# One exponential, one clamp and one sum over 2048 columns per attention step of a gated cross-attention and expert kernel

## The chip, the cores and the metric

The kernel runs on one core of one Trainium2 chip. The metric is the device time of one execution in microseconds. The engines are named as in the profile: PE (TensorE; PEld its weight loads), DVE (VectorE), ACT (ScalarE), POOL (GpSimd), SP (SyncE, which only issues DMAs here).

## The reference

Four sequences of 512 tokens with 256 features (`x`) attend to four contexts of 1024 rows (`ctx_1024`), with 16 heads of 64; then a mixture of four experts, two for each token, follows. Cut to what matters:

```python
q = (lat @ Wq)...                       # lat: layer norm of layer norm of x
k, v = jnp.split(ctx @ Wkv, 2, axis=-1)
k = apply_rope(k, cos, sin)
attn = jnp.einsum('bhnd,bhsd->bhns', q, k) * 64 ** -0.5
attn = jnp.clip(attn, -11.0, 11.0)
attn = jax.nn.softmax(attn, axis=-1)
out = jnp.einsum('bhns,bhsd->bhnd', attn, v)
x = x + tanh(g_xattn) * (out @ Wo + bo)
x = x + tanh(g_ffn) * experts(layernorm(x))     # top 2 of 4, exact gelu
```

All tensors are float32. The kernel takes the exponential of the scores as they are, and clamps the result between exp(-11) and exp(11), which is the same as clipping the scores before it.

## The kernel before

**Tiling.** Each of the four images `b` has four units `u` of four heads. A unit has eight steps `s`. A step treats one pair of heads (`s // 4`) and two tiles of 128 context rows (`2 * (s % 4)` and the next). Its scores are two bank groups `sc[0]` and `sc[1]`, one for each row tile `i`; each holds 128 context rows by 2 heads x 512 tokens, so 1024 columns. There are 4 x 4 x 8 = 128 steps. `c = s % 4` counts the steps of a pair of heads.

**What one step does, in the order of each engine's own program** (each engine works strictly in order; semaphores join them):

- PE (`step` in the tensor block): `score` for i = 0 and i = 1 (L1800, six matmuls each); `k_turn` (L1786), which transposes the rotated keys of the previous row tile of the next unit; `kv_make` (L1745 to L1747), which projects keys and values of one more row tile for the next unit; at c = 0 `denominators` (L1824), which needs the sums of the four steps before; at some steps the output projection or the next queries; then `values` (L1814) of the step before. In about a third of the steps (those that also transpose context or query rows, L1752) `kv_make` stands ahead of `k_turn`.
- ACT: `exps` for i = 0 and 1 (L932), then `kv_evac` (L877 `k_raw`, L878 `val`), then `k_split` (L870).
- DVE: `clamp` for i = 0 and 1 (L1159), then `rot_cos` (L1147), `k_low` (L1111), then `sums` for i = 0 and 1 (L1171 at c = 1, L1174 at c = 2 and 3, none at c = 0), with small steps of other work between and behind.
- POOL: `rotate`, which is two instructions, L716 (`rot_s`, needs `k_raw`) and L720 (the sum of both halves of the rotation, needs `rot_cos` too). The next `k_turn` on PE waits for L720.

`prob` is double buffered over the steps (`s % 2`), `sc` is not: `score` of the next step waits until the exponential has read its half. The semaphores `sc_ready`, `exp_done`, `clamped` and `summed` exist once for each half. In the last unit of the last image (`is_direct`) no sums are made; PE sums the probabilities itself.

The sums that are two instructions of 1024 columns:

```python
            def sums(b, u, s, i):
                ...
                dve.wait_ge(clamped[i], step_no(b, u, s) + 1)
                if c == 1:
                    wait(dve, den_ready, q)
                    v.tensor_tensor(acc[:, i, :], prob[:, 0, i, :], prob[:, 1, i, :], ALU.add).then_inc(summed[i], 1)
```

After the attention the experts run in 19 jobs of 256 tokens; the change touches them only in two waits.

Of the kernel before, what the change touches and what calls it, by code (L numbers as in the profile page):

```python
# [32 lines left out]
def flamingo_kernel(nc, x, ctx_in, g_xattn, g_ffn, cos, sin, lat_g, lat_b, ctx_g, ctx_b, w_q, w_kv, w_o, b_o,  # L33
# [29 lines left out]
    with ExitStack() as stack:  # L63
# [134 lines left out]
        sc = [ps("sc0", 2 * N), ps("sc1", 2 * N)]  # L198
# [65 lines left out]
        sc_ready = [sem("sc_ready0"), sem("sc_ready1")]  # L264
        exp_done = [sem("exp_done0"), sem("exp_done1")]
        clamped = [sem("clamped0"), sem("clamped1")]
        summed = [sem("summed0"), sem("summed1")]
# [592 lines left out]
        def _(act):  # L860
# [123 lines left out]
            def step(b, u, s, last):  # L984
# [3 lines left out]
                exps(b, u, s, 0)  # L988
                exps(b, u, s, 1)
# [90 lines left out]
        def _(dve):  # L1080
# [75 lines left out]
            def clamp(b, u, s, i):  # L1156

                dve.wait_ge(exp_done[i], step_no(b, u, s) + 1)
                v.tensor_scalar(prob[:, s % 2, i, :], prob[:, s % 2, i, :], EXP_LOW, EXP_HIGH,  # L1159
                                ALU.max, ALU.min).then_inc(clamped[i], 1)  # L1160

            def sums(b, u, s, i):
# [78 lines left out]
            def step(b, u, s, last):  # L1241
# [28 lines left out]
                clamp(b, u, s, 0)  # L1270
# [7 lines left out]
                clamp(b, u, s, 1)  # L1278
# [461 lines left out]
        def _(pe):  # L1740
# [48 lines left out]
            def score(b, u, s, i):  # L1789
# [6 lines left out]
                wait(pe, exp_done[i], step_no(b, u, s))  # L1796
# [5 lines left out]
                last.then_inc(sc_ready[i], 1)  # L1802

            def values(b, u, s):
                c, j, p = s % CH, s // CH, u * 2 + s // CH
                if c == 0:

                    wait(pe, o_norm, pair_no(b, p))
                for i in range(2):
                    pe.wait_ge(clamped[i], step_no(b, u, s) + 1)  # L1810
                    for g in range(4):
                        half, h = g // 2, g % 2
                        at = (2 * j + h) * DH + half * 32
                        last = mm(pv[g * 32:(g + 1) * 32, :], val[:, u % 2, 2 * c + i, at:at + 32],  # L1814
                                  prob[:, s % 2, i, h * N:(h + 1) * N], start=c == 0 and i == 0, stop=c == CH - 1 and i == 1)
# [174 lines left out]
            def hidden(n):  # L1990
# [103 lines left out]
```

## Time and profile before

| | before |
|---|---|
| median of 3 runs | 1129.91 us (1127.69 to 1133.77) |
| the profiled execution | 1131.16 us |
| its span | 1129.6 us |
| PE, DVE, ACT, POOL busy | 95%, 84%, 58%, 48% of the span |
| granted TensorE clock, mean | 0.989 of full speed |
| attention steps | about 39 to 850 us of the span |

Busy is the time in which an instruction of the engine is in flight. Times in the rows are microseconds from the start of the span, unless marked ns. The span is the time from the first to the last instruction; the execution's own time is 1.6 us longer.

### The profile page before, as it was taken

The page shows a single profiled execution, that of the slowest core. Times are in us where ns is not written, and L with a number is a line of the kernel's source. Part 1 is how long each engine was busy: PE and PEld are TensorE (multiplying, and loading weights), DVE is VectorE, ACT ScalarE, POOL GpSimd, SP SyncE. Part 2 cuts the span into 40 slices and gives each one's busy share as a digit, 9 for nine tenths or more (in the row PEclk, how much of TensorE's full clock was granted, in tenths as well). Part 3 has the DMA queues.
Part 4 walks back from the last instruction along what each step waited for, and adds up shares of the span by engine and source line. Part 5 has one row for each costly group of instructions (what it writes and reads, how often), then busy time and mean ns, then how long its engine had stood idle before and what let it go on. Part 6 is the DMA issues. An engine that isn't in the chain of part 4 may idle for free.

```text
span 1129.6 us, 22455 instructions
## 1 busy us (share of the span) xinstructions
PE 1070.9 (95%) x7949; PEld 713.9 (63%) x7949; DVE 948.4 (84%) x1772; ACT 653.1 (58%) x1259; POOL 540.6 (48%) x551
## 2 busy tenths in 40 slices
PE   5899999999999999999999999999998998799994
PEld 3556555655555565656555565655447997799994
DVE  7898999898889989898998989889976657577675
ACT  5654557655555765555566655444565764567662
POOL 7433475333427633242654334318832646555661
PEclk9999999999999999999999999999999999999998
DMA  7000010000000000000010000601353334545344
GB/s 208 13 10 11 20 38 20 11 10 11 11 19 25 24 12 10 20 10 20 20 29 10 10 14 7 202 1 54 109 192 121 140 113 132 170 151 170 113 149 142
DMA packets 59188, 72.04 MB, mean 64 GB/s; under 512 B 11579, under 2 KB 52167, under 8 KB 59080
## 3 DMA queue, kind: packets, MB, share of 16 engines
q1 hardware_dynamic: 54840, 61.30, 17.5%
q0 software_dynamic: 3360, 8.53, 2.0%
q8 instruction: 66, 1.08, 0.4%
q10 hardware_dynamic: 880, 0.79, 0.2%
q14 instruction: 42, 0.34, 0.1%
HBM read 54.84 MB, written 16.54 MB: 63 GB/s over the span
## 4 chain that ended last, share of the span: by engine, by line
PE 74%; DVE 13%; issue 5%; ACT 3%; POOL 2%; DMA 1%; SPq 0%; ACTq 0%; DVEq 0%; POOLq 0%
PE pv L1814 16%; PE sc L1800 14%; PE kv L1745 5%; PE kv L1747 5%; PE kv L1746 5%; PE sc L1745 4%; PE sc L1747 4%; PE sc L1746 4%; PE tr L1786 3%; PE mi L1745 2%; DVE acc L1174 2%; PE mi L1746 2%; PE mi L1747 2%; PE mi L1824 2%; DVE prob L1159 2%
## 5 line engine op out<-in xcount | busy, mean ns | idle before, releaser
L932 ACT ACTIVATE prob<-sc 128x1024 f32<-128x1024 f32 x256 | 249.5, 1028 | 200.4 <-PE sc L1800 197.5
L716 POOL TENSOR_TENSOR rot_s<-k_raw,sinb 128x256 f32<-128x256 f32 x128 | 112.7, 880 | 381.1 <-ACT k_raw L877 380.9
L1814 PE MATMUL pv<-prob,val 128*32 128x512 f32 x2048 | 245.5, 597 | 2.3 <-DVE recip L1193 2.3
L1159 DVE TENSOR_SCALAR prob<-prob 128x1024 f32<-128x1024 f32 x256 | 181.6, 722 | 43.9 <-ACT prob L932 42.3
L1800 PE MATMUL sc<-q_hid,w2all 64*128 64x512 f32 x1536 | 213.4, 410 | 1.2 <-DVE w2all L1139 1.2
L1800 PEld LDWEIGHTS sc<-q_hid,w2all 64*128 64x128 f32 x1536 | 135.1, 185 | 101.4 <-issue 55.1
L1174 DVE TENSOR_TENSOR acc<-acc,prob 128x1024 f32<-128x1024 f32 x120 | 177.4, 1499 | 0.0
L720 POOL TENSOR_TENSOR rot_c<-rot_c,rot_s 128x256 f32<-128x256 f32 x128 | 111.6, 872 | 37.6 <-DVE rot_c L1147 23.0
L1814 PEld LDWEIGHTS pv<-prob,val 128*32 128x32 f32 x2048 | 56.5, 109 | 111.2 <-issue 90.4
L1745 PE MATMUL kv<-w2all,acts 128*128 128x512 f32 x248 | 109.8, 443 | 2.2 <-DVE acts L1105 1.3
L1745 PE MATMUL sc<-w2all,q_hid 128*128 x304 | 89.8, 295 | 18.1 <-DVE q_hid L1647 17.4
L1747 PE MATMUL kv<-w2all,acts 128*128 128x512 f32 x248 | 98.5, 397 | 0.0
L1746 PE MATMUL kv<-w2all,acts 128*128 128x512 f32 x248 | 98.0, 395 | 0.0
L1746 PE MATMUL sc<-w2all,q_hid 128*128 x304 | 86.7, 285 | 0.0
L1747 PE MATMUL sc<-w2all,q_hid 128*128 x304 | 86.6, 285 | 0.0
L1171 DVE TENSOR_TENSOR acc<-prob 128x1024 f32<-128x1024 f32 x60 | 85.4, 1461 | 0.0
L877 ACT ACTIVATE k_raw<-kv 128x256 f32<-128x256 f32 x124 | 48.7, 392 | 53.8 <-PE kv L1747 51.4
L1147 DVE TENSOR_TENSOR rot_c<-kv,cosb 128x256 f32<-128x256 f32 x124 | 52.2, 421 | 28.5 <-ACT val L878 22.9
L1745 PEld LDWEIGHTS sc<-w2all,q_hid 128*128 128x128 f32 x304 | 58.7, 193 | 21.4 <-issue 21.2
L779 POOL TENSOR_TENSOR acts<-prob,acts 128x512 fp32r<-128x512 f32 x36 | 48.3, 1343 | 42.8 <-ACT acts L955 41.1
L1030 ACT ACTIVATE sc<-sc,c_aff 128x256 f32<-128x256 f32 x78 | 34.9, 447 | 50.6 <-PE sc L1747 50.1
L1786 PE MATMUL tr<-ident,rot_c 128*128 128x128 f32 x256 | 54.5, 295 | 8.9 <-POOL rot_c L720 8.8
(315 smaller groups left out, 2377.4 us busy)
## 6 DMA issues: line engine op xcount, KB each, us to landing
prob<-in_L_ffn_w SPq DMA_DIRECT2D x17, 1024.0 KB, 5.3
slots_x<-lat_r SPq DMA_DIRECT2D x1, 5016.0 KB, 18.8
rows<-slots_x SPq DMA_DIRECT2D x19, 264.0 KB, 4.4
rows<-in_ctx SPq DMA_DIRECT2D x32, 128.0 KB, 2.2
w_raw<-in_L_xattn_Wq SPq DMA_DIRECT2D x16, 256.0 KB, 2.7
w_raw<-in_L_xattn_Wo SPq DMA_DIRECT2D x64, 64.0 KB
acc<-in_L_ffn_w SPq DMA_DIRECT2D x16, 256.0 KB, 4.0
acc<-in_L_ffn_w SPq DMA_DIRECT2D x5, 512.0 KB
```

Source lines behind the costliest of these rows:

```text
L716: g.tensor_tensor(rot_s[:].rearrange("p (h a c) -> p h a c", h=4, a=2), kh[:, :, ::-1, :], sinb[:, t].unsqueeze(1).to_broadcast([P, 4, 2, ...
L720: g.tensor_tensor(k_rot[:], rot_c[:], rot_s[:], ALU.add).then_inc(rot, 1)
L932: a.activation(prob[:, s % 2, i, :], sc[i][:], ACT.Exp, scale=DH ** -0.5).then_inc(exp_done[i], 1)
L1159: v.tensor_scalar(prob[:, s % 2, i, :], prob[:, s % 2, i, :], EXP_LOW, EXP_HIGH, ALU.max, ALU.min).then_inc(clamped[i], 1)
L1171: v.tensor_tensor(acc[:, i, :], prob[:, 0, i, :], prob[:, 1, i, :], ALU.add).then_inc(summed[i], 1)
L1174: v.tensor_tensor(acc[:, i, :], acc[:, i, :], prob[:, s % 2, i, :], ALU.add).then_inc(summed[i], 1)
L1745: mm(dst, lhs(0), rhs(0), start=start, stop=False, **kw)
L1746: mm(dst, lhs(0), rhs(1), start=False, stop=False, **kw)
L1747: return mm(dst, lhs(1), rhs(0), start=False, stop=stop, **kw)
L1786: last = nc.tensor.transpose(tr[:, j * P:(j + 1) * P], k_rot[:, j * P:(j + 1) * P], ident[:])
L1800: last = mm(sc[i][:, h * N:(h + 1) * N], kst[rows_h, u % 2, j, lk, t * P:(t + 1) * P], q_sp[rows_h, p % 2, lq, :], start=lk + lq == 0, sto ...
L1814: last = mm(pv[g * 32:(g + 1) * 32, :], val[:, u % 2, 2 * c + i, at:at + 32], prob[:, s % 2, i, h * N:(h + 1) * N], start=c == 0 and i == ...
```

## The change

The two score halves become halves of one PSUM tensor of four banks. ACT takes one exponential over 2048 columns, which waits until both halves of the scores are there. DVE clamps 2048 columns in one instruction and adds 2048 columns in one instruction. Each of the four semaphore pairs becomes one semaphore. PE waits for the whole exponential before either half of the next scores, for the whole clamp before `values`, for the whole sum before `denominators`. In the order of DVE the merged clamp stands where the second one stood (behind the small aggregates), and the merged sum where the first one stood (ahead of `residual`).

```diff
-        sc = [ps("sc0", 2 * N), ps("sc1", 2 * N)]
+        scores = ps("scores", 4 * N)
+        sc = [scores[:, 0:2 * N], scores[:, 2 * N:4 * N]]
...
-            def exps(b, u, s, i):
-                act.wait_ge(sc_ready[i], step_no(b, u, s) + 1)
+            def exps(b, u, s):
+                act.wait_ge(sc_ready, 2 * step_no(b, u, s) + 2)
...
-                a.activation(prob[:, s % 2, i, :], sc[i][:], ACT.Exp, scale=DH ** -0.5).then_inc(exp_done[i], 1)
+                a.activation(prob[:, s % 2].rearrange("p i n -> p (i n)"), scores[:], ACT.Exp,
+                             scale=DH ** -0.5).then_inc(exp_done, 1)
...
-                exps(b, u, s, 0)
-                exps(b, u, s, 1)
+                exps(b, u, s)
...
-            def clamp(b, u, s, i):
+            def clamp(b, u, s):
+                dve.wait_ge(exp_done, step_no(b, u, s) + 1)
+                both = prob[:, s % 2].rearrange("p i n -> p (i n)")
+                v.tensor_scalar(both, both, EXP_LOW, EXP_HIGH, ALU.max, ALU.min).then_inc(clamped, 1)
...
-                    v.tensor_tensor(acc[:, i, :], prob[:, 0, i, :], prob[:, 1, i, :], ALU.add).then_inc(summed[i], 1)
+                    v.tensor_tensor(acc[:], prob[:, 0], prob[:, 1], ALU.add).then_inc(summed, 1)
...
-                    v.tensor_tensor(acc[:, i, :], acc[:, i, :], prob[:, s % 2, i, :], ALU.add).then_inc(summed[i], 1)
+                    v.tensor_tensor(acc[:], acc[:], prob[:, s % 2], ALU.add).then_inc(summed, 1)
...
-                clamp(b, u, s, 0)
                 if done_rows:
...
-                clamp(b, u, s, 1)
+                clamp(b, u, s)
...
-                sums(b, u, s, 0)
+                sums(b, u, s)
                 if s in (2, 3) and not is_first(b, u):
                     residual(*((b, u - 1) if u else (b - 1, UNITS - 1)), s - 2)
-                sums(b, u, s, 1)
...
-                wait(pe, exp_done[i], step_no(b, u, s))
+                wait(pe, exp_done, step_no(b, u, s))
...
+                pe.wait_ge(clamped, step_no(b, u, s) + 1)
                 for i in range(2):
-                    pe.wait_ge(clamped[i], step_no(b, u, s) + 1)
...
+                pe.wait_ge(summed, (pair_no(b, p) + 1) * 3)
                 for i in range(2):
-                    pe.wait_ge(summed[i], (pair_no(b, p) + 1) * 3)
```

## Rows read from the trace of the kernel before

**Rows 1.** The page: busy us, share of span and instructions of each engine.

```profile
PE 1070.9 (95%) x7949; PEld 713.9 (63%) x7949; DVE 948.4 (84%) x1772; ACT 653.1 (58%) x1259; POOL 540.6 (48%) x551
```

**Rows 2.** Busy by stretch, attention: length, PE, PEld, DVE, ACT, POOL, clock, DMA, GB/s.

```profile
39.00:245.00 206.00, 204.37 (x1468) 116.48 (x1468) 185.90 (x312) 122.12 (x231) 90.05 (x98) 1.00 0.05 15
...
450.00:655.00 205.00, 203.97 (x1476) 117.33 (x1472) 187.38 (x322) 119.61 (x226) 92.24 (x98) 1.00 0.06 17
655.00:850.00 195.00, 187.46 (x1430) 106.75 (x1430) 170.46 (x300) 103.90 (x167) 93.56 (x83) 0.99 0.28 88
```

**Rows 3.** Waits, attention (39 to 853): us in total, times, longest.

```profile
PEld tr L1752 <- DVE w2all L1111: 7.2, 6, 1.4
PE tr L1786 <- POOL rot_c L720: 5.7, 9, 1.4
```

**Rows 4.** Timeline, all engines, image 2, unit 1, steps 6 and 7: start, us, engine.

```profile
534.60 1.67 PE L1800 MATMUL sc<-q_hid,w2all 64*128 64x512 f32 x12
535.62 1.94 ACT L932 ACTIVATE prob<-sc 128x1024 f32<-128x1024 f32 x2 [2.17 <-PE sc L1800]
...
537.94 0.65 DVE L1159 TENSOR_SCALAR prob<-prob 128x1024 f32<-128x1024 f32 x1
...
538.07 0.39 ACT L877 ACTIVATE k_raw<-kv 128x256 f32<-128x256 f32 x1 [0.51 <-PE kv L1747]
...
538.53 0.74 POOL L716 TENSOR_TENSOR rot_s<-k_raw,sinb 128x256 f32<-128x256 f32 x1 [4.95 <-ACT k_raw L877]
...
539.17 0.41 DVE L1111 TENSOR_TENSOR w2all<-tr,w2all 128x256 fp32r<-128x256 f32 x1
539.42 0.73 POOL L720 TENSOR_TENSOR rot_c<-rot_c,rot_s 128x256 f32<-128x256 f32 x1
539.50 2.87 DVE L1174 TENSOR_TENSOR acc<-acc,prob 128x1024 f32<-128x1024 f32 x2
539.82 1.65 PE L1800 MATMUL sc<-q_hid,w2all 64*128 64x512 f32 x12
...
541.40 0.44 PE L1786 MATMUL tr<-ident,rot_c 128*128 128x128 f32 x2
...
542.29 1.28 DVE L1159 TENSOR_SCALAR prob<-prob 128x1024 f32<-128x1024 f32 x2
```

**Rows 5.** The page's costliest groups: busy us, mean ns of one, idle before, releaser.

```profile
L932 ACT ACTIVATE prob<-sc 128x1024 f32<-128x1024 f32 x256 | 249.5, 1028 | 200.4 <-PE sc L1800 197.5
...
L1159 DVE TENSOR_SCALAR prob<-prob 128x1024 f32<-128x1024 f32 x256 | 181.6, 722 | 43.9 <-ACT prob L932 42.3
```

**Rows 6.** Timeline of POOL, image 1, unit 2, step 1.

```profile
350.34 1.19 POOL L716 TENSOR_TENSOR rot_s<-k_raw,sinb 128x256 f32<-128x256 f32 x1
351.67 1.65 POOL L720 TENSOR_TENSOR rot_c<-rot_c,rot_s 128x256 f32<-128x256 f32 x1
```

**Rows 7.** Timeline of DVE in the same step.

```profile
349.22 1.71 DVE L1159 TENSOR_SCALAR prob<-prob 128x1024 f32<-128x1024 f32 x1
...
351.52 1.21 DVE L1171 TENSOR_TENSOR acc<-prob 128x1024 f32<-128x1024 f32 x1
```

**Rows 8.** Timeline of PE, image 2, unit 0: scores of steps 3 to 6.

```profile
463.37 1.65 PE L1800 MATMUL sc<-q_hid,w2all 64*128 64x512 f32 x12
...
470.00 1.65 PE L1800 MATMUL sc<-q_hid,w2all 64*128 64x512 f32 x12
...
476.07 1.67 PE L1800 MATMUL sc<-q_hid,w2all 64*128 64x512 f32 x12
...
482.65 1.67 PE L1800 MATMUL sc<-q_hid,w2all 64*128 64x512 f32 x12
```

**Rows 9.** Timeline of POOL, image 2, unit 0, step 7: the reciprocal root of L727.

```profile
490.02 2.25 POOL L727 TENSOR_TENSOR f_stats<-f_stats,mhalf 128x4 f32<-128x4 f32 x1
```

**Rows 10.** Timeline of PE, image 1, unit 2, step 0: scores and denominators.

```profile
340.03 1.66 PE L1800 MATMUL sc<-q_hid,w2all 64*128 64x512 f32 x12
...
343.38 1.07 PE L1824 MATMUL mi<-acc,ones 128*32 128x256 f32 x16
```

More of the change, by code:

```diff
@@ L262, in flamingo_kernel @@
         q_ready = sem("q_ready")
[L264 to L267, printed above, removed]
+        sc_ready = sem("sc_ready")
+        exp_done = sem("exp_done")
+        clamped = sem("clamped")
+        summed = sem("summed")
         pv_done = sem("pv_done")
@@ L924, in q_round @@
                 a.activation(q_sp[:, p % 2, 0, :], mi[:], ACT.Copy).then_inc(q_high, 1)
-            def exps(b, u, s, i):
-                act.wait_ge(sc_ready[i], step_no(b, u, s) + 1)
+            def exps(b, u, s):
+                act.wait_ge(sc_ready, 2 * step_no(b, u, s) + 2)
                 c, q = s % CH, pair_no(b, u * 2 + s // CH)
                 if not (is_direct(b, u) and s > 1):
-                    wait(act, summed[i], q * 3 - 1 if c == 0 else q * 3 if c == 1 else q * 3 + 1)
-                a.activation(prob[:, s % 2, i, :], sc[i][:], ACT.Exp, scale=DH ** -0.5).then_inc(exp_done[i], 1)
+                    wait(act, summed, q * 3 - 1 if c == 0 else q * 3 if c == 1 else q * 3 + 1)
+                a.activation(prob[:, s % 2].rearrange("p i n -> p (i n)"), scores[:], ACT.Exp,
+                             scale=DH ** -0.5).then_inc(exp_done, 1)
             def x_out(b, hf, bank, raw):
@@ L1154, in q_low, with sums @@
                 v.tensor_tensor(q_sp[:, p % 2, 1, :], mi[:], q_sp[:, p % 2, 0, :].bitcast(F32), ALU.subtract).then_inc(q_ready, 1)
-            def clamp(b, u, s, i):
[L1158 to L1162, printed above, removed]
+            def clamp(b, u, s):
+                dve.wait_ge(exp_done, step_no(b, u, s) + 1)
+                both = prob[:, s % 2].rearrange("p i n -> p (i n)")
+                v.tensor_scalar(both, both, EXP_LOW, EXP_HIGH, ALU.max, ALU.min).then_inc(clamped, 1)
+            def sums(b, u, s):
                 c, q = s % CH, pair_no(b, u * 2 + s // CH)
@@ L1166, in sums @@
                     return
-                dve.wait_ge(clamped[i], step_no(b, u, s) + 1)
+                dve.wait_ge(clamped, step_no(b, u, s) + 1)
                 if c == 1:
                     wait(dve, den_ready, q)
-                    v.tensor_tensor(acc[:, i, :], prob[:, 0, i, :], prob[:, 1, i, :], ALU.add).then_inc(summed[i], 1)
+                    v.tensor_tensor(acc[:], prob[:, 0], prob[:, 1], ALU.add).then_inc(summed, 1)
                 else:
-                    dve.wait_ge(summed[i], q * 3 + c - 1)
-                    v.tensor_tensor(acc[:, i, :], acc[:, i, :], prob[:, s % 2, i, :], ALU.add).then_inc(summed[i], 1)
+                    dve.wait_ge(summed, q * 3 + c - 1)
+                    v.tensor_tensor(acc[:], acc[:], prob[:, s % 2], ALU.add).then_inc(summed, 1)
             def reciprocals(b, p):
@@ L1801, in score @@
                                   q_sp[rows_h, p % 2, lq, :], start=lk + lq == 0, stop=lk == 1)
-                last.then_inc(sc_ready[i], 1)
+                last.then_inc(sc_ready, 1)
             def values(b, u, s):
@@ L2000, in hidden @@
                 if n in (1, 2):
-                    pe.wait_ge(exp_done[0], B * BS)
+                    pe.wait_ge(exp_done, B * BS)
                 if n == 3:
-                    pe.wait_ge(exp_done[1], B * BS)
+                    pe.wait_ge(exp_done, B * BS)
                 if n == 11:
```

## The prediction

> **What bounds the kernel now.** I read the page first: PE is busy for 95% of the span, DVE for 84% [rows 1]. Then the stretches [rows 2]: over the attention (39 to 850 us) PE lacks 1.6, 1.0, 1.0 and 7.5 us of four stretches (the second, not shown, repeats the third), 11.2 us in all, at a clock of 0.99 to 1.00. DVE is at 90% and more in the first three. So PE sets the time, and everything else counts only by what it makes PE wait for. The third view is the list of waits [rows 3]: PE waits for L720 on POOL and L1111 on DVE, a few times, little. Both are links of the key chain: keys projected on PE, copied by ACT (L877), rotated by POOL (L716), DVE and POOL again (L720), then transposed by PE (L1786) in the next step. The fourth view is the timeline of one step, to see how much room that chain has [rows 4]. The step starts at T = 534.60; the second clamp ends at T+3.99; L877 starts at T+3.47, L716 at T+3.93, L1111 at T+4.57, L720 at T+4.82 and it ends at T+5.55. PE wants it at 541.40, T+6.80, in the next step. The room is 1.25 us, in the shortest kind of step (5.22 us).
>
> **Exponential.** Two instructions take 1.94 us back to back [rows 4]; one alone 1.03 [rows 5]. One over 2048 columns cannot be longer than 1.94, and saves at most the part that is not columns; I take 1.88 (ends 1.75 and 1.94). ACT saves some 128 x 0.06 = 8 us busy, worth nothing: it idles 197.5 us before L932 for PE alone [rows 5]. What counts is the start. It now waits for both halves: half of the 12 matmuls, some 0.70 us, later than T+1.02. So it runs from T+1.72 to T+3.60; the second one of before ended at T+2.96. PE wants the banks again at T+5.22 at the earliest here [rows 4], so the single bank group costs PE nothing. L877 stands behind the exponential on ACT: it moves from T+3.47 to about T+3.50, L716 to T+3.97.
>
> **Clamp.** A pair takes 1.28 us [rows 4]; merged 1.24 (ends 1.20 and 1.28). It starts at T+3.63 instead of half way through the exponentials and ends at T+4.87, 0.88 later than before. PE reads it a step later, so `values` doesn't wait.
>
> **The collision.** L716 now asks to start at T+3.97, while the clamp runs; before, the clamp was all but over. The trace of before has this case with 1024 columns [rows 6, 7]: the clamp ends at 350.93, L716, started at 350.34, takes 1.19 instead of 0.74 and ends 0.60 behind the clamp. DVE gets through L1147 and L1111 (which read PSUM) and starts the sum L1171 at 351.52, 0.59 behind the clamp's end. L720 starts at 351.67, 0.74 behind it: 0.15 too late. It takes 1.65 us instead of 0.73 and ends at 353.32, 0.59 behind the end of that sum (352.73). In the step of [rows 4] the order is the other way round: L720 is first by 0.08 us, takes 0.73, and the sums are stretched (2.87 for two, 1.21 alone).
>
> So whichever starts first keeps the other out until it ends. The merged clamp makes this order happen in every step with sums that is not one of the long ones, and the merged sum is twice as long. From T: clamp ends 4.87, sum starts 5.46, runs 2.30 (twice 1.21 less what is not columns; ends 2.25 and 2.42) to 7.76, L720 ends at 8.35, PE can start L1786 at 8.40. It wanted it at 6.82 behind a step of 5.22: a wait of 1.58 us of PE.
>
> The Trainium skill (page "SBUF — State Buffer", section "Who interferes with whom") says that VectorE and GpSimd share a port pair, that the first to issue holds it for the whole instruction and the other blocks fully, and that a VectorE instruction with two SBUF inputs or in a two-port mode takes part. The trace agrees for 1024 columns (the 0.60 and 0.59 above); that a hold of 2048 columns lasts 2.3 us no run here shows. By a sharing of bandwidth instead, L720 would be some 0.5 us late and the total would end near the second rival.
>
> **Which steps pay.** With c = 0 there are no sums: L720 is then only 0.7 late and has room. The steps with `kv_make` ahead of `k_turn` ask for L720 1.5 us later, after steps of 6 to 8 us: room. That leaves, with step lengths of 6.63 (from 463.37), 6.58 (from 476.07) [rows 8] and 5.22:
> - behind a step of 6.58: wanted at 8.18, waits 0.22; behind 6.63: 0.17.
> - behind step 6 of a unit (5.22, already lengthened by 0.22 of wait): 1.36. Without that lengthening: 1.58.
> - behind step 7: nothing. PE's wait has moved `kv_make` 1.4 later, L877 comes when the clamp is over, and L720 is again ahead of the sum. One wait also makes its own step longer, so that two small ones never follow each other.
>
> Unit 0 pays 0.22 + 0.17 + 0.22 + 1.36 = 1.97, unit 1 (two of its steps are long) 1.75, unit 3 (its second half) 1.58, unit 2 is nearly all of the long kind: 5.3 us an image. Image 0 has no projections in unit 0: 2 x 1.58 + 1.75 + 1.58 = 6.5. In image 3 unit 0 pays 1.97 and unit 1 about 0.9; its later units wait for DVE anyway. Sum 6.5 + 5.3 + 5.3 + 2.9 = 20.0 us.
>
> **The rest.** Where context rows are transposed, L1111 is wanted in the same step and PE waits for it already [rows 3]; it comes 0.4 to 0.6 later in one of two places and L720 0.4 in another: 0.7 x 3 = 2.1 us. L727 and its companion stand between two L720 on POOL [rows 9], once in each of three images, at least 2.25 us: they start 2 us later; 0.5 x 3 = 1.5 (ends 0 and 3 x 2). `denominators` now waits for the whole sum. PE comes to it 3.35 into a step [rows 10]; the sums of a step of 5.22 end 2.55 into the next [rows 4], now 0.6 later or less; nothing. The last unit, without sums, carries the 0.64 of the exponential at its waits for DVE: 0.7. Against it, where PE waits for a DVE that is never idle (unit 2 of image 3, 8 steps), DVE saves 0.04 of a clamp and 0.12 of a sum a step: -1.3. Together 3.0.
>
> **Sum.** 1131.16 + 20.0 + 3.0 = 1154.2 for the profiled execution; it lies 1.25 above the median of the runs, so 1153 on the scale of 1129.91. 2.0% slower.
>
> **Rivals.**
> 1. It goes further: a POOL that is held off for 2.3 us at a time also delays its other small work (norm scales, low parts of weights), in the long steps as well, and DVE is held off by POOL at its merged clamp. Each of some 90 steps with sums could add 0.2 more: 1171. For it: L727 took 2.25 us [rows 9]. Against: the long steps have 2.5 us of room. Chance 0.13.
> 2. L720 is not late, because it wins against the sum after all (it loses by only 0.15 us), or a long instruction gives way. Then only the 0.6 to 0.9 of later exponential and clamp remain, which the room of 1.25 covers; 2 to 3 us are left: 1132. Against: in [rows 6, 7] both instructions hang on the same clamp's end, so the 0.15 doesn't depend on its length. Chance 0.15.
> 3. The other side: faster. DVE sheds 128 x 0.04 + 90 x 0.12 = 16 us busy and ACT 8. PE's idle time in the attention is 11.2 us [rows 2], of which 7.5 in the last stretch, where DVE is what it waits for. If DVE's shorter program moves those waits forward and the early steps keep their room, half of it comes back: 1124. It decides the sign if the sum of waits at L1786 grows by less than 5 us. The Trainium skill (page "VectorE: DVE Perf Modes", section on the trn2 errata) speaks for it: a fixed cost per instruction, so larger tiles pay it less often; its formula gives 2.29 us for an add of 2048. Chance 0.07.
>
> That PE waits for the exponential, as the scores now have one bank group, I leave at nothing: 3.60 against 5.22. Only the last unit, without keys to make, has shorter steps.
>
> **How the numbers follow.** Forecast 0.65, its own range 1145 to 1162 (the bounds of the sum and clamp, and 0 to 6 for L727). Rival 1 0.13, rival 2 0.15, rival 3 0.07. A measurement of this kernel tells 0.5%, 5.6 us, from no change. Slower by more: forecast, rival 1 and a small part of rival 2, 0.80. Within: 0.13. Faster: 0.07. The range reaches down toward rival 2 and up into rival 1: 1136 to 1169.
>
> **What would show it.** Right: L716 in the short steps takes over 1.2 us and ends 0.6 behind the clamp; L720 takes about 2.8 us where it took 0.73, and ends 0.6 behind the sum; waits of PE for L720 grow from 5.7 to over 20 us, the longest runs of them in step 7 of units 0, 1 and 3, 1.4 us each; clamp 1.24, sum 2.30, exponential 1.88; DVE's busy time falls although the span grows. Wrong: L720 stays at 0.74 in the median with the steps at 5.22 (rival 2); waits spread over unit 2 (rival 1); a score matmul that waits for L932 (the bank group after all).

## The result and the profile after

| | before | after |
|---|---|---|
| median of 4 runs | 1130.99 us (1127.69 to 1133.77) | 1158.70 us (1155.67 to 1161.77) |
| the profiled execution, its span | 1131.16, 1129.6 us | 1158.52, 1156.9 us |
| first score to last score | 808.98 us | 835.76 us |
| ahead of it, behind it | 39.01, 281.57 us | 39.33, 281.83 us |

The changed kernel is slower: ratio 1.0246, interval 1.0206 to 1.0286. Nearly all of it arises in the attention, 26.8 of the 27.4 us by which the profiled execution is longer. The lines of kernel.py have moved by one or two: L716 and L720 (the rotation on POOL) are L717 and L721 after, L1786 (k_turn) is L1785, L932 is L933, L1159 is L1161, L1174 is L1175. Below, a step's length is the time from its first score matmul to that of the next step; "image 2, unit 1, step 7" is written 2/1/7.

The page of after, busy time of each engine, and its groups (columns as in [rows 1] and [rows 5]):

```profile
PE 1076.2 (93%) x7949; PEld 716.1 (62%) x7949; DVE 905.6 (78%) x1554; ACT 641.5 (55%) x1131; POOL 687.5 (59%) x551
...
L933 ACT ACTIVATE prob<-scores 128x2048 f32<-128x2048 f32 x128 | 241.0, 1883 | 269.7 <-PE scores L1799 264.3
L717 POOL TENSOR_TENSOR rot_s<-k_raw,sinb 128x256 f32<-128x256 f32 x128 | 166.9, 1304 | 272.4 <-ACT k_raw L878 272.2
L1161 DVE TENSOR_SCALAR prob<-prob 128x2048 f32<-128x2048 f32 x128 | 159.8, 1248 | 133.5 <-ACT prob L933 132.0
L721 POOL TENSOR_TENSOR rot_c<-rot_c,rot_s 128x256 f32<-128x256 f32 x128 | 207.0, 1617 | 25.3 <-DVE rot_c L1148 8.1
```

DVE does 43 us less than in [rows 1], ACT 12 us less; POOL is 147 us longer in flight with the same 551 instructions. Each merged instruction is cheaper than its pair was: exponential and clamp by [rows 5] and the groups above, and the sums took 262.8 us in 180 instructions before (L1171 and L1174) and take 224.1 us in 90 after (L1172 and L1175). But the two instructions of the rotation now take POOL 2.92 us a step (1304 and 1617 ns); before they took 1.75 (880 and 872 ns), and 0.74 and 0.73 where nothing held them off ([rows 4]).

Stretches of the attention after, to be read beside [rows 2]: PE now lacks 7.7, 5.8, 6.3 and 13.2 us, 33.0 in all; before it was 11.2. So 21.8 of the 26.8 us are time in which PE stands still. The other 5.0 are longer times of PE's own instructions, some 3 us of them at a lower clock in two steps, 0/0/0 and 3/2/7.

```profile
39.30:244.00 204.70, 197.01 (x1392) 112.58 (x1392) 165.56 (x243) 113.99 (x190) 124.02 (x93) 0.99 0.05 15
244.00:450.00 206.00, 200.23 (x1441) 115.43 (x1442) 171.91 (x261) 114.38 (x191) 129.19 (x96) 1.00 0.06 17
450.00:660.00 210.00, 203.66 (x1469) 116.43 (x1467) 175.59 (x264) 115.91 (x194) 132.59 (x97) 1.00 0.06 16
660.00:875.10 215.10, 201.92 (x1526) 113.69 (x1524) 172.68 (x265) 108.07 (x148) 130.46 (x90) 0.98 0.24 77
```

What it waits for, from the list of waits after (39 to 880; before, the second line was 5.7 us in 9 waits, [rows 3]):

```profile
PEld tr L1785 <- POOL rot_c L721: 47.1, 51, 2.9
PE tr L1785 <- POOL rot_c L721: 23.8, 20, 2.4
```

These waits grow by 18.1 us. All that PE waits for DVE grows by less than 2 in the same list, and no wait of PE for the exponential (L933) is in it. The same two steps as in [rows 4], 2/1/6 and 2/1/7, timeline of all engines after:

```profile
551.97 1.67 PE L1799 MATMUL scores<-q_hid,w2all 64*128 64x512 f32 x12
...
553.68 1.88 ACT L933 ACTIVATE prob<-scores 128x2048 f32<-128x2048 f32 x1 [2.86 <-PE scores L1799]
...
555.60 1.23 DVE L1161 TENSOR_SCALAR prob<-prob 128x2048 f32<-128x2048 f32 x1 [0.32 <-ACT prob L933]
...
556.10 1.33 POOL L717 TENSOR_TENSOR rot_s<-k_raw,sinb 128x256 f32<-128x256 f32 x1 [2.38 <-ACT k_raw L878]
...
557.38 1.65 PE L1799 MATMUL scores<-q_hid,w2all 64*128 64x512 f32 x12
...
557.40 2.28 DVE L1175 TENSOR_TENSOR acc<-acc,prob 128x2048 f32<-128x2048 f32 x1
557.57 2.70 POOL L721 TENSOR_TENSOR rot_c<-rot_c,rot_s 128x256 f32<-128x256 f32 x1
...
560.32 0.44 PE L1785 MATMUL tr<-ident,rot_c 128*128 128x128 f32 x2 [1.28 <-POOL rot_c L721]
```

With T = 551.97: exponential T+1.71, clamp T+3.63 to T+4.86, L717 asks inside it and ends at 557.43, 0.60 behind its end. The sum starts at 557.40; L721, at 557.57, is 0.17 late and ends at 560.27, 0.59 behind the sum. k_turn starts 0.05 after that. Step 7 takes 1.35 us more than before.

In the trace, 54 of the 128 L721 take over 2.6 us and 66 under 0.9. Before, 108 of the 128 L720 took under 0.9 and none over 2.

### The profile page after: what moved, and what is told of

It reads as the page before. It is cut to its first block, busy times and chain, and to the rows that moved or that the text cites. A ratio compares the mean times of both kernels' runs of the same rounds, so it can differ in the third digit from the quotient of the medians.

```text
span 1156.9 us, 21858 instructions
## 1 busy us (share of the span) xinstructions
PE 1076.2 (93%) x7949; PEld 716.1 (62%) x7949; DVE 905.6 (78%) x1554; ACT 641.5 (55%) x1131; POOL 687.5 (59%) x551
## 4 chain that ended last, share of the span: by engine, by line
PE 61%; POOL 15%; DVE 9%; issue 7%; ACT 5%; DMA 2%; SPq 0%; POOLq 0%; DVEq 0%; ACTq 0%
PE pv L1813 11%; PE scores L1799 11%; POOL rot_c L721 8%; PE kv L1744 5%; POOL rot_s L717 4%; PE kv L1746 4%; PE kv L1745 4%; PE scores L1744 4%; PE scores L1746 3%; PE scores L1745 3%; PE tr L1785 3%; ACT prob L933 2%; PE mi L1823 2%; PE mi L1744 2%; DVE prob L1161 1%
## 5 line engine op out<-in xcount | busy, mean ns | idle before, releaser
L933 ACT ACTIVATE prob<-scores 128x2048 f32<-128x2048 f32 x128 | 241.0, 1883 | 269.7 <-PE scores L1799 264.3
L717 POOL TENSOR_TENSOR rot_s<-k_raw,sinb 128x256 f32<-128x256 f32 x128 | 166.9, 1304 | 272.4 <-ACT k_raw L878 272.2
L1161 DVE TENSOR_SCALAR prob<-prob 128x2048 f32<-128x2048 f32 x128 | 159.8, 1248 | 133.5 <-ACT prob L933 132.0
L721 POOL TENSOR_TENSOR rot_c<-rot_c,rot_s 128x256 f32<-128x256 f32 x128 | 207.0, 1617 | 25.3 <-DVE rot_c L1148 8.1
L1799 PE MATMUL scores<-q_hid,w2all 64*128 64x512 f32 x1536 | 214.6, 411 | 1.2 <-DVE w2all L1140 1.2
L1799 PEld LDWEIGHTS scores<-q_hid,w2all 64*128 64x128 f32 x1536 | 135.6, 186 | 102.1 <-issue 54.5
L1175 DVE TENSOR_TENSOR acc<-acc,prob 128x2048 f32<-128x2048 f32 x60 | 151.2, 2520 | 0.0
L1744 PE MATMUL scores<-w2all,q_hid 128*128 x304 | 89.8, 296 | 17.5 <-DVE q_hid L1646 17.1
L1745 PE MATMUL scores<-w2all,q_hid 128*128 x304 | 86.8, 286 | 0.0
L1746 PE MATMUL scores<-w2all,q_hid 128*128 x304 | 86.5, 285 | 0.0
L1785 PE MATMUL tr<-ident,rot_c 128*128 128x128 f32 x256 | 54.5, 295 | 29.8 <-POOL rot_c L721 27.6
L1172 DVE TENSOR_TENSOR acc<-prob 128x2048 f32<-128x2048 f32 x30 | 72.9, 2429 | 0.0
L1785 PEld LDWEIGHTS tr<-ident,rot_c 128*128 128x128 f32 x256 | 29.5, 145 | 68.2 <-POOL rot_c L721 51.8
L1744 PEld LDWEIGHTS scores<-w2all,q_hid 128*128 128x128 f32 x304 | 58.6, 193 | 20.8 <-issue 20.6
```

Of the source, the lines that this page charges most:

```text
L717: g.tensor_tensor(rot_s[:].rearrange("p (h a c) -> p h a c", h=4, a=2), kh[:, :, ::-1, :], sinb[:, t].unsqueeze(1).to_broadcast([P, 4, 2, ...
L721: g.tensor_tensor(k_rot[:], rot_c[:], rot_s[:], ALU.add).then_inc(rot, 1)
L933: a.activation(prob[:, s % 2].rearrange("p i n -> p (i n)"), scores[:], ACT.Exp, scale=DH ** -0.5).then_inc(exp_done, 1)
L1161: v.tensor_scalar(both, both, EXP_LOW, EXP_HIGH, ALU.max, ALU.min).then_inc(clamped, 1)
L1172: v.tensor_tensor(acc[:], prob[:, 0], prob[:, 1], ALU.add).then_inc(summed, 1)
L1175: v.tensor_tensor(acc[:], acc[:], prob[:, s % 2], ALU.add).then_inc(summed, 1)
```

## The experiments

Two theories. **A**: the late clamp puts the rotation's second instruction on POOL behind the sum, the merged sum shuts it out for 2.3 us, and PE waits for it in k_turn. **B**: something else that came with the merge: one bank group, DVE's later order, or the merged sum wherever it stands. "Attention" is the growth from first to last score against the profile of before; ratios are against before on the same chip. The ranges of the expectations are on the scale of before at 1131 us (1130.99); a ratio times that puts a run on this scale. Each attention length is from one profile, and falls of the clock move it by 1.5 to 2 us each (last section).

| kernel | exp | clamp | sum | other | attention, us | ratio |
|---|---|---|---|---|---|---|
| after | 1 | 1 | 1 | | +26.8 | 1.0246 (1.0206 to 1.0286) |
| g1 | 1 | 1 | 2 | | +14.6 | 1.0137 (1.0089 to 1.0185) |
| g2 | 1 | 1 | 512 + 1536 | | +11.9 | 1.0112 (1.0064 to 1.0159) |
| g3 | 1 | 2 | 1 | | +40.1 | 1.0376 (1.0327 to 1.0426) |
| g4 | 1 | 1 | 1 | sum behind the rotation | +30.7 | 1.0253 (1.0203 to 1.0303) |
| h4 | 1 | 1 | 1 | the same, steps 6, 7 only | +14.7 | 1.0159 (1.0118 to 1.0199) |
| h2 | 1 | 1 | 1 | kv_make first | +15.9 | 1.0141 (1.0100 to 1.0181) |
| k2 | 1 | 1 | 1 | rotation's add on DVE | +13.5 | 1.0155 (1.0122 to 1.0188) |
| h1 | 2 | 2 | 1 | | +2.0 | 1.0027 (1.0005 to 1.0048) |
| k1 | 2 | 1 | 2 | | +3.8 | 1.0026 (1.0003 to 1.0050) |
| h3 | 2 | 2 | 2 | kv_make first | +2.0 | 1.0029 (1.0010 to 1.0049) |
| k3 | 2 | 2 | 2 | rotation's add on DVE | -1.1 | 0.9994 (0.9978 to 1.0010) |
| m1 | 2 | 2 | 2 | the same, images 0 to 2 | -2.3 | 0.9965 (0.9949 to 0.9982) |

### g1 and g2: a shorter hold at the same place

```diff
-v.tensor_tensor(acc[:], prob[:, 0], prob[:, 1], ALU.add)
+for i in range(2):       # g1: 1024 + 1024; g2: columns 0:512, then 512:2048
+    v.tensor_tensor(acc[:, i, :], prob[:, 0, i, :], prob[:, 1, i, :], ALU.add)
```

(and so at c = 2, 3)

> Of the changed kernel only the merged sum is undone: two adds of 1024 columns in its place, one semaphore. Theory A (whoever of DVE and POOL starts first keeps the other out until its instruction ends; L721 loses to the sum by 0.15 us): L721 is held off by the first add only, 1.21 us instead of 2.28, and ends 1.07 us earlier; it then takes 1.65 us. Behind a step of 5.22 us PE waits 0.4 to 0.5 us instead of 1.36, behind 6.58 nothing. Image 2 takes about 1.6 us longer than before instead of 6.1, the whole about 1141 (1138 to 1145), 17 us less than the changed kernel. Theory B (the chain is late because the exponential and the clamp end later; the length of the sum has no part in it): within 2 us of the changed kernel, 1157 to 1160. Theory C (POOL and DVE share a bandwidth): L721 as slow as before, since two adds move the same bytes; 1155 to 1160.

> As the changed kernel, but the sum in two adds of 512 and 1536 columns, the short one first. Theory A: L721 is held off by 0.68 us of add and ends at T+6.75 of a step, 0.07 before PE wants it behind the shortest step: it takes 1.1 to 1.2 us, PE waits for next to nothing in steps 7; the whole 1135 to 1139. It is the third point of a line with 1024 and 2048 columns held. Theory B and C: as for the split into halves, 1155 to 1160.

Medians 1143.34 and 1139.62 us, before 1127.71. L721 in 2/1/6, timelines of g1 and then of g2:

```profile
549.00 2.88 DVE L1178 TENSOR_TENSOR acc<-acc,prob 128x1024 f32<-128x1024 f32 x2
549.15 1.65 POOL L721 TENSOR_TENSOR rot_c<-rot_c,rot_s 128x256 f32<-128x256 f32 x1
```

```profile
546.46 2.90 DVE L1181 TENSOR_TENSOR acc<-acc,prob 128x512 f32<-128x512 f32 x2
546.61 1.13 POOL L721 TENSOR_TENSOR rot_c<-rot_c,rot_s 128x256 f32<-128x256 f32 x1
```

L721 ends 0.6 us behind the first sum, whatever comes behind that: it takes 2.70, 1.65, 1.13 us for 2048, 1024, 512 columns. Step 2/1/7 grows by 1.35, 0.62 and 0.09. For the hold and its cost in step 7 that is theory A, and B (the length of the sum has no part) and C (a shared bandwidth) are out. The totals are not in the sizes expected: on the scale of 1131 they are 1146.5 and 1143.7 us, above A's ranges (to 1145 and to 1139), image 2 grows by 3.6 us in g1 where 1.6 was expected, and half of the loss stays. In g1, 8.8 of its 14.6 us are still waits at k_turn for POOL (14.5 us in 21 waits), in g2 3.8 of 11.9 (9.5 in 10).

### g3: two clamps, so that POOL gets in between

```diff
-v.tensor_scalar(both, both, EXP_LOW, EXP_HIGH, ALU.max, ALU.min).then_inc(clamped, 1)
+for i in range(2):
+    half = both[:, i * 2 * N:(i + 1) * 2 * N]
+    last = v.tensor_scalar(half, half, EXP_LOW, EXP_HIGH, ALU.max, ALU.min)
+last.then_inc(clamped, 1)
```

> As the changed kernel, but the clamp in two instructions of 1024 columns, both behind the one exponential of 2048. Theory A: L717 asks while the first clamp runs. If it gets in between the two, it ends before the second clamp does, L721 needs only L1148 and starts 0.08 us ahead of the merged sum: 0.74 us in the median, no waits in steps 7, about 1135 (1132 to 1140). If the two clamps hold the port without a gap, nothing changes: 1157 to 1161 with L717 at 1.3 us. Theory B: DVE's clamps end 0.04 us later than the merged one or more, so 1158 to 1163 either way.

1169.66 us: slower than after, and outside every expectation. Timeline of g3, 2/1/5 to 2/1/7:

```profile
556.62 2.71 DVE L1175 TENSOR_TENSOR acc<-prob 128x2048 f32<-128x2048 f32 x1
...
559.42 1.88 ACT L933 ACTIVATE prob<-scores 128x2048 f32<-128x2048 f32 x1 [3.43 <-DVE acc L1175]
...
561.34 1.83 DVE L1163 TENSOR_SCALAR prob<-prob 128x1024 f32<-128x1024 f32 x2 [0.39 <-ACT prob L933]
561.65 0.96 POOL L717 TENSOR_TENSOR rot_s<-k_raw,sinb 128x256 f32<-128x256 f32 x1 [4.47 <-ACT k_raw L878]
...
563.58 0.73 POOL L721 TENSOR_TENSOR rot_c<-rot_c,rot_s 128x256 f32<-128x256 f32 x1 [0.97 <-DVE rot_c L1148]
563.75 2.71 DVE L1178 TENSOR_TENSOR acc<-acc,prob 128x2048 f32<-128x2048 f32 x1
```

The order does turn round: L717 gets in between the clamps, L721 is first and takes 0.73. But now DVE is held off, twice a step (clamps 1.83 instead of 1.28 for a pair, sum 2.71 instead of 2.28), and DVE has something of its own on the path: the exponential of step 6 writes the half of `prob` that the sum of step 5 reads, so L933 waits for it. In 24 steps of g3 it starts over 0.25 us behind the end of its scores for this reason, in after in one. This is a second constraint, which neither theory had. PE still waits 20.2 us in 25 waits at k_turn for POOL, though L721 itself takes 0.79 us in the mean, and 8.6 us in 9 waits for L1112: the chain is late as a whole.

### g4 and h4: DVE waits for POOL

```diff
 dve.wait_ge(clamped, step_no(b, u, s) + 1)
+if not (b == B - 1 and u >= 2):          # g4; h4 adds: and s in (6, 7)
+    dve.wait_ge(rot, kv_no(*next_unit(b, u), s) + 1)
```

> As the changed kernel, all instructions kept at their sizes; only the sum on DVE also waits until L721 of the same step has ended (images 0 to 2, and units 0 and 1 of image 3). It adds a wait and takes none away. Theory A: L721 always starts ahead of the sum and takes 0.74 us, PE's waits in steps 7 and at the start of unit 1 go; the sum comes 0.9 us later, for which DVE has room except ahead of the denominators (0.1 to 0.2 us each). 1134 to 1142, some 20 us less than the changed kernel. Theory B: a wait more on the same chain cannot help; DVE is later still, 1158 to 1168.

> The changed kernel; DVE's merged sum waits for POOL's second instruction of the rotation (so POOL is always first at the port), but only in steps 6 and 7 of a unit, not in all steps as in g4, and not in the last two units. Steps 6 and 7 set the largest waits (1.36 us in step 7, 1.53 in step 0 of unit 1, some 11 of them), and there no exponential waits for the sum one step later and no residual stands behind it. Theory A (g4 failed because the sum it put off was also wanted by the next exponential and by the residual): 1145 (1141 to 1150), no L933 waiting for a sum. Theory B (any sum put off by 0.9 us comes back on DVE as a later clamp and the next collision): 1153 to 1160.

g4: 1155.80 us, by its ratio 1159.6 on the scale of 1131 and so in B's range. Theory A's number is missed though the waits it speaks of shrink (L721's mean is 0.84 us, the steps 7 of units 0, 1 and 3 of images 0 to 2 grow by 1.4 us together instead of 9.5). The timeline of g4 around 2/1/6, and a line of its waits, show the same second constraint:

```profile
551.91 2.29 DVE L1174 TENSOR_TENSOR acc<-prob 128x2048 f32<-128x2048 f32 x1 [0.89 <-issue]
...
554.30 1.88 ACT L933 ACTIVATE prob<-scores 128x2048 f32<-128x2048 f32 x1 [3.38 <-DVE acc L1174]
```

```profile
ACT prob L933 <- DVE acc L1174: 57.2, 17, 3.8
```

The exponential starts late for this reason in 17 steps of g4. PE pays in `denominators`, where it waits 6.8 us in 12 waits for a sum and 3.1 in 7 for the residual (L1207); in after it has no such wait.

h4 puts off only sums that no exponential waits for a step later: 1143.23 us (before 1126.62), by its ratio 1149 (1144 to 1153.5) on the scale of 1131. A expected 1145 (1141 to 1150); B's range, 1153 to 1160, is just touched by the interval. The same steps 7 grow by nothing in sum (after: 9.5 us), and one exponential is late, as in after. So the gain of the right order is real, and g4 lost it in the other steps, the ones whose sums the next exponential or `denominators` wants.

### h2 and h3: the reader of the rotation later

```diff
-if make and turned:
+if make:
     kv_make(nb, nu, s)
...
-if make and not turned:      # behind k_turn
-    kv_make(nb, nu, s)
```

> The changed kernel with one edit on PE: kv_make stands ahead of k_turn in every step, where before it did so in a third of them. The transposes of the rotated keys are then wanted some 1.5 us later in the short steps. Theory A (the whole loss is k_turn waiting for POOL's second instruction behind the merged sum): that instruction still takes about 2.7 us in most steps, but nobody waits for it; the waits of 1.36 and 1.53 us go, what stays is the part of the steps that had this order already (about 0.8 us an image, and 2 in image 3): 1136 (1132 to 1140). Theory B (the hold costs by what it does to DVE's and ACT's own order): it stays at 1150 to 1160. Theory C (the wait only moves on: keys split later, DVE's subtraction of the low part later, the sum later, the clamp later): 1142 to 1150, with DVE late at L1112.

> The kernel before with the same one edit on PE (kv_make ahead of k_turn in every step). It has only 5.7 us of waits at k_turn for POOL, most of them in steps of the order that is changed here. Theory A: 1127 (1124 to 1131), a gain of 0 to 5 us over before. Theory C (the later k_turn delays the low part of the keys on DVE, which is 84% busy): 1131 to 1138, slower than before. The difference between h2 and h3 is what the change costs when k_turn is out of reach: by A 5 to 9 us, by B 20 or more.

h2: 1141.02 us, between A and C; by its ratio 1147 (1142 to 1151) on the scale of 1131, which is C's range and not A's. The wait for L1112 that C named did not grow, though: 2.3 us in 6, as in after. The timeline of h2 in 2/1/6 and 2/1/7 (T = 541.67; k_turn stands at T+3.1 in it, at T+1.8 in after):

```profile
547.09 2.28 DVE L1175 TENSOR_TENSOR acc<-acc,prob 128x2048 f32<-128x2048 f32 x1
547.24 2.73 POOL L721 TENSOR_TENSOR rot_c<-rot_c,rot_s 128x256 f32<-128x256 f32 x1
```

L721 takes 2.73 us as in after and ends at 549.97, but k_turn is due only then, 3.1 us into the next step, and step 7 grows by 0.13 instead of 1.35. This separates the hold from its reader: here the hold alone costs nothing. What stays is mainly +1.0 in steps 2/2/2 and 2/1/0 and their like in the other images (L726 in the second), and 7.3 us in units 2 and 3 of image 3, where k_turn waits for POOL twice more (1.6 and 3.8 us) and the clock falls in 3/3/5. h3, the same edit on before, is 1.0029: it has nothing to win there, and of its +2.0 us 1.55 are in the very first step (the last section has the reason). h2 less h3 is 14 us in the attention: more than A's 5 to 9.

### h1 and k1: one merge alone

```diff
# h1, on before                          # k1, on before
-sums(b, u, s, 0); sums(b, u, s, 1)      -clamp(b, u, s, 0); clamp(b, u, s, 1)
+sums(b, u, s)                           +clamp(b, u, s)      # waits for both exp_done
```

> The kernel before with one edit: the two sums of a step become one of 2048 columns, at the place of the first; exponentials and clamps stay two each of 1024. Theory A (the long sum costs only where the rotation's second instruction comes behind it, and it is the later clamp that puts it there in most steps): here the clamp ends as early as before, so POOL's second instruction is still first in the short steps and keeps its 0.73 us; the loss is in the few places where it lost already against a sum of 1024 (it then waits for 2.3 instead of 1.2 us): about six to eight of them, 1.1 us each, so 1138 (1134 to 1142), with L720's mean under 1.1 us. Theory B (the merged sum is bad wherever it stands, the clamp has no part in it): 1150 to 1158.

> The kernel before with one edit: the two clamps of a step become one of 2048 columns at the place of the second (it waits for both exponentials of 1024). Exponentials and sums stay two each. By the times of a short step before, the clamp then starts at T+3.0 and ends at T+4.23, 0.24 later than the second clamp did; POOL's first instruction, asking at T+3.93, is held off for 0.3 and ends 0.6 behind the clamp, its second starts 0.15 behind the first sum, but that one is only 1.2 us long, so it ends at T+6.6 and k_turn wants it at T+6.8. Theory A (what makes the clamp late is the exponential over both halves, which starts 0.7 later): 1128 (1125 to 1132), little or no loss, though L720's mean rises over 1.2 us. Theory B (it is the merged clamp itself that does what g1 lost): 1137 to 1144.

h1: 1129.22 against 1126.62 us, which is 1134.0 us on the scale of 1131, the lower end of A's range; B's 1150 is excluded. k1: 1137.21 against 1134.05, on that scale 1133.9 (1131 to 1137), between A's range (to 1132) and B's (from 1137). Each merge alone makes 0.3%, by the intervals at most 0.5%. Timelines of h1 and k1 in 2/1/6:

```profile
541.26 0.73 POOL L720 TENSOR_TENSOR rot_c<-rot_c,rot_s 128x256 f32<-128x256 f32 x1
541.36 2.78 DVE L1175 TENSOR_TENSOR acc<-acc,prob 128x2048 f32<-128x2048 f32 x1
```

```profile
539.14 1.23 DVE L1161 TENSOR_SCALAR prob<-prob 128x2048 f32<-128x2048 f32 x1 [0.23 <-ACT prob L932]
...
540.98 2.90 DVE L1175 TENSOR_TENSOR acc<-acc,prob 128x1024 f32<-128x1024 f32 x2
541.11 1.69 POOL L720 TENSOR_TENSOR rot_c<-rot_c,rot_s 128x256 f32<-128x256 f32 x1
```

In h1 POOL is first by 0.10 us. In k1 the order is the bad one in 52 steps, but the hold is 1.2 us and starts early: L720 ends at 542.80, and k_turn starts at 542.88, when it would have started anyway. Sum and clamp merged alone make +2.0 and +3.8; with the exponential merged as well, clamp and exponential make +14.6 and all three +26.8. The costs do not add. That each takes of the same 1.25 us of room is how I explain it. The exponential alone was not run, nor sum and clamp together without it; g1 against k1 puts its merge at some 11 us on top of the clamp's.

### k2, k3 and m1: the add on DVE

```diff
 # POOL, rotate: only rot_s = k_raw * sin
-g.tensor_tensor(k_rot[:], rot_c[:], rot_s[:], ALU.add).then_inc(rot, 1)
 # DVE, behind k_low, ahead of the sum
+dve.wait_ge(rot1, kv_no(b, u, t) + 1)
+dve.wait_ge(rot2, kv_no(b, u, t) + 1)
+v.tensor_tensor(k_rot[:], rot_c[:], rot_s[:], ALU.add).then_inc(rot, 1)
```

> The changed kernel with one edit: the rotation's second instruction (k_rot = rot_c + rot_s) moves from POOL to DVE, between k_low and the sum, where DVE's own order keeps it ahead of the sum. Theory A (the loss is POOL's second instruction shut out by the merged sum): rot_s ends 0.6 behind the clamp, T+5.5, the add takes some 0.42 us on DVE (as L1148 and L1112 do for 256 columns) and ends at T+5.95, ahead of T+6.8 where k_turn wants it; the sum ends at T+8.2, the next clamp can start at T+8.85. No waits for a rotation in the attention but for small ones: 1129 (1125 to 1135), DVE busy 950 to 965 us. Theory B (the real limit is DVE's order behind the late clamp: another 0.4 us there pushes sums into the next exponential, the residual and the denominators, as in g4): 1140 to 1156.

> The kernel before with the same one edit (k_rot's add on DVE). The collision is rare there, and DVE, at 90% and more over most of the attention, gets 54 us more work. Theory A: it becomes DVE's in places: 1134 (1128 to 1145), slower than k2, which has 40 us less on DVE for the merged instructions. If k3 is as fast as k2 or faster, the merged instructions are worth nothing even with the collision gone.

> A candidate to beat both kernels: the kernel before (two instructions each of 1024 columns) with k_rot's add on DVE in the attention steps of images 0 to 2 only; the keys made before the attention and those of image 3's steps keep it on POOL. In k3 the attention of images 0 to 2 was 1.2 us shorter each than before, the stretch ahead of the first score 3.0 us longer (DVE is the busier engine there) and image 3 2.6 us longer. Theory A (the three add up by place): 3.7 us less than before, ratio 0.997 (0.995 to 0.999), first score at 39.0 us again. Theory B (the gains of k3 are paid back in image 3 or in the tail whatever that image does): ratio 0.999 to 1.001.

k2: 1149.63 against 1134.05 us. The collision is gone: in 2/1/6 the add (L1153) takes its turn on DVE,

```profile
550.51 0.43 DVE L1153 TENSOR_TENSOR rot_c<-rot_c,rot_s 128x256 f32<-128x256 f32 x1
550.86 2.28 DVE L1177 TENSOR_TENSOR acc<-acc,prob 128x2048 f32<-128x2048 f32 x1
```

and the steps 7 of units 0, 1 and 3 of images 0 to 2 grow by 0.02 us in sum. Theory A's 1129 (1125 to 1135) is missed all the same, and B's range (1140 to 1156: another 0.4 us on DVE pushes its other work into what waits for it) is met: 3.0 us are ahead of the first score (the keys made there also got the add on the busier engine), 13.5 in the attention, where PE has no wait for POOL's rotation left. From the list of waits of k2 (39 to 880), PE waits for DVE now: for q_hid, in the turns of context rows (L1757), in `denominators` and in k_turn:

```profile
PE mi L1750 <- DVE q_hid L1157: 4.5, 4, 1.2
PE tr L1757 <- DVE w2all L1109: 3.8, 9, 0.5
PE mi L1829 <- DVE acc L1177: 3.7, 5, 1.9
...
PE tr L1791 <- DVE rot_c L1153: 3.2, 7, 0.9
```

So taking the collision away gives back about half of the loss of after. The other half is not the same loss left over: most of these waits are new in k2. In after PE waited 1.4 us for q_hid, 2.3 in the context turns and not at all in `denominators`. k2 has the late clamp and one more add on DVE; k3 shows that the add costs nothing where the clamp is early. The late clamp alone, without collision and without the add, was not run.

k3, 1133.29 us, is as fast as before, and 16 us faster than k2: with the rotation's add on DVE in both, the merged instructions still only cost. m1 keeps POOL's add ahead of the attention and in image 3: 1129.75 us (1125.88 to 1131.62) against 1133.35 (1131.87 to 1137.28). That is the version that beats both, before by 0.35%, where 0.3% was expected. (Its attention is 2.3 us shorter in the profile, not 3.7. Images 0 to 2 have -4.1, as expected. Image 3 has +1.8: the clock gives -1.5 in step 3/1/5 and takes +1.5 in 3/3/5, and 3/2/5 and 3/3/0 have +0.8 and +0.9.)

## Why the prediction was right

1153 us (1136 to 1169) was forecast, 1158.7 measured; 1153 is 2.0% over before, measured are 2.5%. By its own steps:

- **Times in a step.** Exponential 1.88 (1.883), its start T+1.72 (T+1.71), the clamp to T+4.87 (T+4.86), clamp 1.24 (1.25), sum 2.30 (2.28), L717 and L721 ending 0.60 and 0.59 behind DVE's instruction: all as said. L717 was taken as 1.5 us and is 1.33 here (1.50 in the median). The Trainium skill (page "SBUF — State Buffer", section "Who interferes with whom") has the first to issue hold the shared port for its whole instruction; the trace agrees for 2048 columns too (2.70 us, and 1.65 and 1.13 in g1 and g2). A sharing of bandwidth, by which the sum would have come near rival 2, is excluded by the length of L721, which follows the first sum alone.
- **DVE's busy time.** It was to shed 16 us and sheds 43. The 16 came from instructions in their undisturbed lengths; before, POOL held off many of the pairs (L1174 took 1499 ns in the mean, L1171 1461, where one alone takes 1.21 us [rows 7]), and the merged ones are held off less. It changed nothing: DVE does not set the time.
- **Which steps pay.** Images 1 and 2 were put at 5.3 and 0.7 (context turns) and 0.5 (L727), 6.5 us; they measure 6.07 and 6.05. Unit 3: 1.58 forecast, 1.55 measured. Inside unit 0 the step failed: 1.97 was forecast, of which 1.36 at step 7, and step 7 grows by nothing. The copy L1374 stands between clamp and rot_cos in step 6 and lets POOL finish first; L721 then is ahead of the sum. The price comes one step later instead, three times what I gave to L727. Timeline after, 2/0/6 to 2/1/0:

```profile
502.92 0.70 DVE L1374 COPY f_stats<-f_stats 128x8 f32<-128x8 f32 x1
...
504.03 0.74 POOL L721 TENSOR_TENSOR rot_c<-rot_c,rot_s 128x256 f32<-128x256 f32 x1 [0.43 <-DVE rot_c L1148]
504.20 2.72 DVE L1175 TENSOR_TENSOR acc<-acc,prob 128x2048 f32<-128x2048 f32 x1
504.73 2.25 POOL L726 TENSOR_TENSOR f_stats<-f_stats,eps 128x4 f32<-128x4 f32 x1
...
507.06 1.38 POOL L728 TENSOR_TENSOR f_stats<-f_stats,mhalf 128x4 f32<-128x4 f32 x1
...
508.05 0.95 POOL L717 TENSOR_TENSOR rot_s<-k_raw,sinb 128x256 f32<-128x256 f32 x1
...
508.98 2.28 DVE L1175 TENSOR_TENSOR acc<-acc,prob 128x2048 f32<-128x2048 f32 x1
509.14 2.71 POOL L721 TENSOR_TENSOR rot_c<-rot_c,rot_s 128x256 f32<-128x256 f32 x1
```

  L721 loses in step 7 because two small instructions on POOL, held off by the sum, stand ahead of L717: +1.53 in step 0 of unit 1, once in each of images 1 to 3. The two errors, 1.36 too much and 1.0 too little, nearly cancel.
- **Image 0.** 7.2 forecast with its context turns, 8.8 measured. The difference is step 0/0/0, +1.52, in which the clock fell: see the last section.
- **Image 3.** 2.9 + 0.5 (L727) - 1.3 + 0.7 = 2.8 forecast, 5.9 measured: the largest miss. In units 0 and 1 it pays 4.0 where 3.4 stood. In units 2 and 3 the gain of a shorter DVE is there (-2.2 in the first four steps of unit 2), but steps 7 and 0 after it cost +4.08 and -1.73: POOL's scatters (L750), a queue I had not priced, stand around L717 and L721, and PE runs at a lower clock behind the wait (0.82 over the step: part of it at the level of 1.2 GHz). The step before it has the one late exponential of after: L933 waits for the sum L1172 until 823.84, 1.0 us behind its scores. Timeline of after in 3/2/7:

```profile
824.93 0.97 POOL L750 DMA_INDIRECT slots_x<-rows,route  x1 [0.30 <-issue]
...
826.08 1.51 POOL L717 TENSOR_TENSOR rot_s<-k_raw,sinb 128x256 f32<-128x256 f32 x1 [0.17 <-issue]
...
827.73 2.70 POOL L721 TENSOR_TENSOR rot_c<-rot_c,rot_s 128x256 f32<-128x256 f32 x1
...
830.48 0.44 PE L1785 MATMUL tr<-ident,rot_c 128*128 128x128 f32 x2 [2.42 <-POOL rot_c L721]
...
832.66 3.11 PE L1813 MATMUL pv<-prob,val 128*32 128x512 f32 x16
```

- **Costed at nothing.** The bank group: right but for one step. The forecast took the steps of the last unit for the only short ones; step 0/0/0 is 3.36 us long before, less than the 3.60 at which the exponential ends. In g1, g2, g3, g4, h2, h4 and k2 the next scores wait 0.3 us for L933 there and the step grows by 0.37; in after, PE is slower in this step and the wait does not show. `denominators`: right in after; in g1, g2, h2, h4 and k2 it became a wait of 1 to 4 us, in g4 a longer one.
- **Rivals.** Rivals 2 and 3 fell with the waits at k_turn. Rival 1 said that every step with sums pays 0.2; only small ones in some steps do (0.13 to 0.19, 17 steps of image 0 to 2).

That images 1 and 2 came out so near is luck in part: two errors of more than 1 us, in unit 0 and at the start of unit 1, cancel in each of them. Of the 3.8 us by which the growth of the attention was put too low (23.0, measured 26.8), 3.1 are image 3's and 1.5 are the clock in step 0/0/0.

The cause as the forecast put it, a room of 1.25 us that the late clamp uses up, is shown by h1, k1 and h2: long sum without late clamp, late clamp without long sum, and both with a later reader. In after itself the waits at k_turn for POOL are 18.1 of the 26.8 us. What the forecast did not see is that repairing the collision doesn't bring the time back: g1, g2, h4, h2 and k2 each remove or shorten the waits in the steps 7, each in another way, and each keeps 12 to 16 us. The lists of waits (39 to 880) say where PE stands still in them:

| PE waits, us | before | after | g1 | g2 | h4 | h2 | k2 |
|---|---|---|---|---|---|---|---|
| at k_turn, for POOL | 5.7 | 23.8 | 14.5 | 9.5 | 10.8 | 7.6 | 0 |
| at k_turn, for DVE | 0 | 0 | 0 | 0 | 0 | 0 | 3.2 |
| other work in the bank of `tr`, for L1112 | 2.0 | 2.8 | 4.3 | 5.1 | 3.8 | 3.4 | 6.6 |
| matmuls into `mi`, for q_hid | 0.9 | 1.4 | 1.2 | 1.1 | 0.9 | 4.4 | 4.5 |
| `denominators` | 0 | 0 | 1.4 | 1.4 | 2.9 | 1.1 | 3.7 |

So up to 9 us of what g1 to h2 keep are still the old wait, in unit 2 and in image 3 above all, and some 2 us in g1, g2, h2 and k2 are a fall of the clock in step 3/3/5. The rest is small waits for DVE in other places. That they come from DVE's later start is how I read it; no run separates it.

## What to carry to other kernels

Merging instructions of an engine that is not the bound saved nothing here; ask first when the merged one starts (it waits for its last input) and for how long it shuts out the neighbour at its port. Where an instruction of POOL with a reader close behind is issued within a few tenths of a DVE instruction, the length of that DVE instruction is what it takes. And when such an edit is tried, try each merge alone: here two of three cost 0.3% each, and together with the third, which was not tried alone, they cost 2.5%.

## What I had not expected of the hardware

- A fall of PE's clock can cost more than the wait ahead of it, and it does not come every time. In after, PE stood still for 1.24 us ahead of its first score at 39.33, as it did before. Before, the clock stayed at 1.00 and the 12 matmuls took 1.66 us; after it fell to the level of 1.2 GHz and they took 2.55. A window of after, columns as in [rows 2]:

```profile
40.00:42.00 2.00, 2.00 (x11) 1.16 (x8) 0.00 (x0) 0.07 (x1) 0.42 (x1) 0.50 0.00 0
```

  That is the 1.52 us of step 0/0/0. It is not the change's: h3, with the exponentials of before, has +1.55 in the same step at a clock of 0.62, and the other kernels with the merged exponential have +0.37 at a clock of 1.00. The same happens in step 3/3/5 behind a wait of PE of 2.6 us in g1, g2, g4, h2 and k2 (+1.9 to +2.0 us; clock 0.67 in g1 and 0.61 in k2 over 4 us) and of 2.3 us in k1 and m1 (+1.7 and +1.5), and not in before, after, h1, h3, h4 and k3, which have the same waits (2.3 to 2.6 us) at a clock of 1.00. A third place is step 3/1/5. There the clock falls in the profile of before itself (8.09 us at a clock of 0.79), in after, g2, g3, g4, h3, k2 and k3 too, and not in g1, h1, h2, h4, k1 and m1 (6.56 to 6.65 us at 1.00). So 1.5 us of what the latter seem to gain on before are not theirs.
- Whoever is held off at the port gets in between two instructions of the other engine: L717 between two clamps (g3), L721 between two sums (g1, k1). A merged instruction takes this gap away; that is what the long hold consists of.
- The time behind the last score is 275.0 to 281.8 us in the profiles of fourteen kernels that hardly differ there, while the lengths of single undisturbed steps agree to 0.01 us. The attention's own length was the sharper measure, but for its falls of the clock.
